# Flamingo-style decoder block: first three attentions with fp32 scores in row groups, a ones column in V, and DMA layout of later queries and keys

## The reference

```python
x = x + tanh(g_xattn[i]) * xattn_i(layernorm(x), ctx)   # i = 0..3
x = x + tanh(g_ffn[i])   * ffn_i(layernorm(x))
```

```python
q = heads((x @ Wq.T + bq) * 8**-0.5)      # attention 0 scales the scores, which is the same
k, v = heads(ctx @ Wk.T + bk), heads(ctx @ Wv.T + bv)
scores = q @ k.T + bias_i                 # 256 x 256 for each head and batch
scores = where(mask, scores, -inf)        # 0: an integer mask per query; 1, 2: key padding
out = (softmax(scores) @ v).merge_heads() @ Wo.T + bo
```

## Time and profile before

| | us |
|---|---|
| median of 3 runs | 860.76 (860.72 to 862.41) |
| profiled execution, its own time | 862.37 |
| its span | 860.4 |
| PE busy | 702.3 (82%) |
| DVE busy | 573.1 (67%) |
| ACT busy | 488.9 (57%) |
| POOL busy | 166.6 (19%) |
| DMA moved | 32.26 MB |

### The profile page before, as it was taken

One profiled execution on the slowest core, in us unless ns is written; L12 is line 12 of the kernel. 1 busy time (PEld: TensorE's weight loads), 2 busy tenths in 40 slices (PEclk: granted clock), 3 DMA queues, 4 the chain that ended last, 5 costly groups with the idle time before them and its releaser, 6 DMA issues. The chain is left out here.

```text
span 860.4 us, 14382 instructions
## 1 busy us (share of the span) xinstructions
PE 702.3 (82%) x4728; PEld 396.0 (46%) x4728; DVE 573.1 (67%) x1765; ACT 488.9 (57%) x1323; POOL 166.6 (19%) x135
## 2 busy tenths in 40 slices
PE   4589994559997878999744899949999999869978
PEld 2266663336665323333222667635336666644322
DVE  3699995869996358667865999855316666436553
ACT  2288881259883568598812988812666556413201
POOL 8622000420000045536655000020000000000000
PEclk8689997769999768998885999979999999969999
DMA  8895004060000000000009200000000000000000
GB/s 310 169 319 177 2 7 69 23 126 2 2 2 2 0 1 0 1 0 1 1 0 180 41 2 2 2 26 0 1 0 1 1 2 2 1 1 1 0 1 24
DMA packets 22056, 32.26 MB, mean 38 GB/s; under 512 B 1760, under 2 KB 15712, under 8 KB 21216
## 3 DMA queue, kind: packets, MB, share of 16 engines
q1 hardware_dynamic: 21984, 31.36, 14.4%
HBM read 21.39 MB, written 9.96 MB: 36 GB/s over the span
## 5 line engine op out<-in xcount | busy, mean ns | idle before, releaser
L816 ACT ACTIVATE RING<-RING,NMX 128x256 f32<-128x256 f32 x384 | 190.7, 500 | 56.2 <-DVE NMX L1637 55.8
L1637 DVE CUSTOM_DVE_ANT_0 RING<-bank,ADJM 128x256 f32<-128x256 f32 x384 | 143.4, 413 | 23.5 <-DMA scratch<-RING 22.5
L1158 PE MATMUL bank<-W,RING 128*128 128x128 f32 x768 | 120.5, 282 | 15.6 <-ACT RING L828 13.9
L541 POOL TENSOR_TENSOR small<-small 128x8 f32<-128x8 f32 (+2 forms) x13 | 17.7, 1365 | 463.1 <-DVE small L1528 463.1
L1158 PEld LDWEIGHTS bank<-W,RING 128*128 128x128 f32 x768 | 91.7, 145 | 27.9 <-ACT RING L816 23.2
L1138 PE MATMUL bank<-ARENA 128*128 128x256 bf16 x384 | 77.8, 290 | 30.7 <-DMA ARENA<-scratch 25.7
L1649 DVE COPY RING<-bank 128x512 f32<-128x512 f32 x144 | 98.6, 686 | 1.2 <-PE bank L1158 0.8
L816 ACT ACTIVATION_READ_ACCUMULATOR RING<-RING,NMX 128x1 f32 x384 | 72.8, 190 | 0.0
L997 PE MATMUL bank<-XT,W 128*128 128x512 f32 (+2 forms) x118 | 62.2, 668 | 6.6 <-ACT XT L712 5.3
L728 ACT ACTIVATE RING<-bank,NMX 128x512 f32<-128x512 f32 x64 | 43.4, 683 | 41.8 <-PE bank L1062 21.2
L1280 PE MATMUL bank<-ARENA,W 64*128 64x512 f32 x180 | 62.3, 710 | 3.6 <-DVE ARENA L1830 2.3
(11 more groups left out here) (253 smaller groups left out, 1307.3 us busy)
## 6 DMA issues: line engine op xcount, KB each, us to landing
scratch<-ARENA SPq DMA_DIRECT2D x18, 256.0 KB, 3.2
ARENA<-scratch SPq DMA_DIRECT2D x6, 768.0 KB, 10.6
W<-in_weights SPq DMA_DIRECT2D x1, 2564.0 KB, 21.2
scratch<-RING SPq DMA_DIRECT2D x36, 64.0 KB, 3.0
ARENA<-scratch SPq DMA_DIRECT2D x12, 192.0 KB, 3.8
scratch<-RING SPq DMA_DIRECT2D x18, 128.0 KB, 2.9
ARENA<-scratch SPq DMA_DIRECT2D x6, 384.0 KB, 6.6
W<-in_weights SPq DMA_DIRECT2D x2, 1024.0 KB, 13.7
```

Source lines behind the costliest of these rows:

```text
L816: nc.scalar.activation(P_OF(n)[:, q * S:(q + 1) * S], S_OF(n)[:, q, :], ACT.Exp, bias=NMX[:, 2 * t + q:2 * t + q + 1], scale=-1.0, accum_o ...
L1158: mm = nc.tensor.transpose(bk[:, o:o + P], P_OF(n)[:, i:i + P], ident)
L1637: nc.vector.tensor_tensor_reduce(out=S_OF(n)[:, q, :], in0=SBANK(n)[:, q * S:(q + 1) * S], in1=ADJM[:, b, q, :], scale=-1.0, scalar=BIG, o ...
```

## The change

- The bf16 parts, the DRAM scratch and all clearing of `QS` and `KS` go. Queries and keys stay fp32 in `QT` and `KT`: a head's 8 features lie in partitions 32j to 32j+7 of group g. The scores of a group for 128 queries are four fp32 products with 8 rows each, at rows 0, 32, 64 and 96, into banks 0 to 3. All four banks are used for one such step and again for the next. A unit `n` is now a pair of heads for 128 queries, so the count of units, of maxima and of exponentials stays.
- The queries and keys of the first 256 tokens (for keys, of attention 0 only) are produced in that layout by PE itself (`heads`, four column groups), with the biases spread by 16 small products (`biases`). Those of the later tokens are plain products into `QC` and `KC`, laid out by DMA within SBUF, 16 transfers of 8 rows (`scatter`). Their products are issued inside the loop at t = 1; V of attentions 0 and 2 at t = 3; the bias row of attention 0 at t = 5.
- V gets a column of ones for each head, so the product with V gives the row sums too. The sums in ACT's exponential go, as do L1654 and L1190. In their place: a copy of the 128 x 256 product by DVE, two transposes, a reciprocal straight from PSUM and a small product on DVE for each group; for each batch two transposes back, a copy by ACT, and one product (and bias row) for each 128 tokens with Wo gathered by 16 DMAs (`compact`).
- The copies of transposed probabilities alternate between DVE and ACT. The products with V are spread, one half of the keys at every other t.
- DVE makes only batch 0 of attention 0's masks ahead of the loop, and the others at t = 6 of the loop (`other_masks`), after a wait for the other masks, the padding and the bias matrices of attentions 1 and 2. Some of POOL's mask work for attentions 1 and 2 moves ahead of their layernorms.
- Keys of attentions 1 and 2, V and the bias row of 1, and the bias row of 2, are made during feed-forward part 0.

```diff
-LAG, PV_T, OTR_T, SEL_T, OUT_T = 3, 8, 9, 13, 27
-PT_SLOTS = 7
+LAG, PV_T, OTR_T, ONE_T, BACK_T, OUT_T, END_T = 3, 7, 9, 11, 25, 29, 14
...
-        QS = ARENA[:, 0:8192].bitcast(BF16).rearrange("p (h t) -> p h t", h=H16)
-        KS = ARENA[:, 8192:12288].bitcast(BF16).rearrange("p (j t) -> p j t", j=H16 // 2)
+        QT = ARENA[:, 0:4096].rearrange("p (g t) -> p g t", g=4)
+        KT = ARENA[:, 4096:8192].rearrange("p (g t) -> p g t", g=4)
+        PT = ARENA[:, 8192:12288].rearrange("p (s j k q) -> p s j k q", s=2, j=4, k=2)
...
-        def SBANK(n):
-            return bank[(0, 1, 7)[n % 3]]
-
         def TBANK(n):
-            return bank[(2, 3, 5)[n % 3]]
+            return bank[4 + n % 2]
...
+            def compact(a):
+
+                at = COL[f"wo{a}"][0]
+                for g in range(NG):
+                    for j in range(HG):
+                        sp.dma_start(WOC[a][PAD * g + DH * j:PAD * g + DH * (j + 1), :],
+                                     w_in[PAD * j:PAD * j + DH, at + g * P:at + (g + 1) * P]).then_inc(s_wo[a], 16)
+
+            def scatter(dst, src, t0, done):
+
+                for g in range(NG):
+                    for j in range(HG):
+                        r = PAD * g + DH * j
+                        sp.dma_start(dst[PAD * j:PAD * j + DH, g, t0:TOK], src[r:r + DH, t0:TOK]).then_inc(done[g], 16)
+
+            compact(0)
+            sp.wait_ge(s_he, NG + 2)
+            scatter(KT, KC[0], S, s_ks)
+            sp.wait_ge(s_ea, QC_AT[0])
+            scatter(QT, QC, S, [s_qs] * NG)
...
+            sp.dma_start(ADJ[:, 1:3, :, :], adj_in[:, 1:3, :, :]).then_inc(s_ldm2, 16)
...
+            sp.wait_ge(s_adjm, B * TPB)
+            compact(1)
+            sp.wait_ge(s_he, NG + 4)
+            scatter(KT, KC[1], 0, s_ks)
+            compact(2)
+            sp.wait_ge(s_ea, QC_AT[1])
+            scatter(QT, QC, S, [s_qs] * NG)
...
+            def clear_values():
+
+                nc.gpsimd.memset(ARENA[:, 14336:14336 + NT * VW], 1.0).then_inc(s_zero, 1)
+
             pool.wait_ge(s_set, 1)
             roots()
+            clear_values()
             pool.wait_ge(s_set, 2)
-            masks(0)
-            for a in (1, 2):
-                for step in range(4):
-                    key_parts(a, step)
+            masks(0, 1, B)
...
-                            nc.scalar.activation(P_OF(n)[:, q * S:(q + 1) * S], S_OF(n)[:, q, :], ACT.Exp,
-                                                 bias=NMX[:, 2 * t + q:2 * t + q + 1], scale=-1.0,
-                                                 accum_out=SUMS[:, 2 * t + q:2 * t + q + 1]
+                            nc.scalar.activation(P_OF(n)[:, i * S:(i + 1) * S], S_OF(n)[:, i, :], ACT.Exp,
+                                                 bias=NMX[:, 2 * t + i:2 * t + i + 1], scale=-1.0
...
+            def heads(out, name, g, rhs):
+
+                for j in range(HG):
+                    f = DH * (HG * g + j)
+                    mm = nc.tensor.matmul(out[PAD * j:PAD * j + PAD, :], w(name, f, f + PAD), rhs, start=True,
+                                          stop=True)
+                return mm
...
+                    if t < UNITS and t % 2 == 0:
+                        m = t // 2
+                        b, g, q = m // 8, m // 2 % 4, m % 2
+                        if q == 0 and b == 0:
+
+                            pe.wait_ge(s_qd if g % 2 else s_qa, 2 * a + g // 2 + 1)
+                            if a > 0:
+                                pe.wait_ge(s_ks[g], 16 * HG * (a + 1))
+                        if m == 8:
+                            pe.wait_ge(s_qs, 16 * H16 * (a + 1))
+                            if a == 0:
+                                for k in range(NG):
+                                    pe.wait_ge(s_ks[k], 16 * HG)
+                        scores.fill(pe, [(s_max, 2 * base + 4 * m + 4)])
+                        for j in range(HG):
+
+                            r = slice(PAD * j, PAD * j + DH)
+                            mm = nc.tensor.matmul(bank[j][:, 0:S], QT[r, g, b * S + q * P:b * S + (q + 1) * P],
+                                                  KT[r, g, b * S:(b + 1) * S], start=True, stop=True)
+                            if j % 2 == 1:
+                                mm.then_inc(s_s, 1)
+                    if t == 1:
+                        later_queries(a)
+                    if a != 1 and t == 3:
+                        values(a, ra, s_fa)
+                    if a == 0 and t == 5:
+                        out_row(0, ra, s_fa)
...
+                        for j in range(HG):
+
+                            f = PITCH * (HG * g + j)
+                            mm = nc.tensor.matmul(bank[6][PAD * j:PAD * j + PAD, 0:S], V[:, 2 * b + part, f:f + PAD],
+                                                  PT[:, GG % 2, j, part, :], start=(part == 0), stop=(part == 1))
...
+                    if t >= ONE_T and (t - ONE_T) % 4 == 0 and (t - ONE_T) // 4 < UNITS // 4:
+
+                        G = (t - ONE_T) // 4
+                        GG, b = base // 4 + G, B * a + G // 4
+                        pe.wait_ge(s_otr, GG + 1)
+                        pe.wait_ge(s_on, GG)
+                        if G % 4 == 0:
+                            pe.wait_ge(s_otn, b)
+                        if G % 4 == 1:
+                            pe.wait_ge(s_res, TPB * b)
+                        for q in range(TPB):
+                            mm = nc.tensor.transpose(bank[7][:, q * P:(q + 1) * P],
+                                                     OTR[:, GG % 2, q * P:(q + 1) * P], ident)
+                        mm.then_inc(s_one, 1)
+                    if t >= BACK_T and (t - BACK_T) % 16 == 0:
+
+                        b = (t - BACK_T) // 16
+                        i = B * a + b
+                        pe.wait_ge(s_on, 4 * i + 4)
+                        for q in range(TPB):
+                            mm = nc.tensor.transpose(bank[7][:, q * P:(q + 1) * P], ON[:, i % 2, q, :], ident)
+                        mm.then_inc(s_back2, 1)
...
+                            nc.tensor.matmul(o, OTN2[:, i % 2, q * P:(q + 1) * P], WOC[a], start=True, stop=False)
+                            mm = nc.tensor.matmul(o, ones_row, BOR[a], start=False, stop=True)
...
+            def other_masks():
+
+                dve.wait_ge(s_ldm2, 48)
+                mask_terms(1, B)
...
+                        if a == 0 and t == 6:
+                            other_masks()
...
+                        src = bank[7][:, 0:S].rearrange("p (q j r) -> p q j r", q=2, j=HG)
+                        link(nc.vector.reciprocal(RS, src[:, :, :, DH:PITCH]))
+                        nc.vector.tensor_tensor(
+                            ON[:, i % 2, :, PAD * g:PAD * g + PAD].rearrange("p q (j d) -> p q j d", j=HG),
+                            src[:, :, :, 0:DH], RS.to_broadcast([P, TPB, HG, DH]), ALU.mult).then_inc(s_on, 1)
...
```

More of the change, by code:

```diff
@@ L473, in write @@
-            def write(side, parts, slots, cut, ready, n_ready, written):
-                rows = scratch[side].rearrange("(h i d) t -> i h d t", h=H16, i=6)
-                for part in range(3):
-                    sp.wait_ge(ready, n_ready + part + 1)
-                    for i in slots[part]:
-                        sp.dma_start(rows[i][:, :, cut], parts[:, part, cut]).then_inc(written, 16)
-            def read(side, dst, cut, written, n_written, done):
-                sp.wait_ge(written, n_written)
-                rows = scratch[side].rearrange("(j e r) t -> e r j t", e=2, r=6 * DH)
-                for e in range(2):
-                    sp.dma_start(dst(e)[:, :, cut], rows[e][:, :, cut]).then_inc(done, 16)
@@ L545, in roots, with masks @@
                 root(TPB, NT)
-            def masks(a):
+            def masks(a, b0, b1):
                 if a > 0:
                     pool.wait_ge(s_max, 2 * UNITS * a)
-                for b in range(B):
+                for b in range(b0, b1):
                     for q in range(TPB):
@@ L609, in _ @@
             nc.gpsimd.partition_all_reduce(AMAXR, AMAX, P, bass.bass_isa.ReduceOp.max).then_inc(s_amr, 1)
+            pool.wait_ge(s_ldm2, 48)
+            masks(1, 0, 2)
             roots()
-            masks(1)
+            masks(1, 2, B)
             root()
@@ L693, in _ @@
             pool.wait_ge(s_int, 2 * NC)
-            clear_queries()
-            clear_rest()
+            clear_values()
             roots()
-            masks(2)
+            masks(2, 2, B)
             root()
@@ L829, in attention @@
[L829 to L837 removed]
+                        if GG >= 2:
+                            act.wait_ge(s_pv, GG - 1)
@@ L1013, in turn, with biases, first_keys, keys @@
                     n_xn[0] += 1
-            def keys(a):
-                for c in range(NC):
-                    product(rk, [(w(f"wk{a}"), CT[:, half(c)])], s_fk)
+            def biases():
+                at = COL["cols"][0] + CI["bk0"][0]
```

(31 more changed lines are left out.)

498 lines of the change are left out of this document (214 added, 284 removed).

## The result

The changed kernel takes 961.48 us (median of four executions, 949.41 to 988.53) against 860.86 beside it. That is 1.107 times the time before, with a 95% interval of 1.101 to 1.113. The forecast was 808 (786 to 838). The executions of the changed kernel differ far more among themselves than those of before, and their time goes with the granted clock (0.839 at 949.41 us, 0.784 at 988.53, and 0.774 in one more of 992.27). The profile shown is of the one of 988.53 us, with a span of 986.7.

What follows compares the result with a forecast made beforehand. DVE was taken to bound the attention loops, before and after. Savings of 13.1, 17.0 and 23.4 us in attentions 0, 1 and 2, less 1 in the feed-forward part, made -52.5 us: median 808 us, range 786 to 838.

Steps and rivals of the forecast that it cites:

- The first maxima at 24, about 160 and about 425 us: Sign of being right: when the loops of attentions 0, 1 and 2 take their first maximum.
- stop at t = 6: Attention 0's loop: DVE waits 9 us for the bias matrices, queued behind scatters, before making the other masks.
- rival 4: Loops: DMA layout late, every loop stops at m = 8, 5 us each; 823 us, chance 0.05.
- the 7.6 to 9.5 given: Ahead of each loop: us from first normalised tile to first maximum, 7.6 at the high clock, otherwise taken as 9.5.
- DVE bounds the loop of the kernel before: Attention loops before the change: DVE has about 21 us of work in a batch of 22.19 us.
- rival 2: Score products: row groups run one after another, 3.9 us a pair; 941 us, slower than before; chance 0.04.
- the step on ACT: Loop: ACT loses 32 accumulator reads a batch (190 ns each) and gains four copies; no gain of its own.
- 2.47 to 2.55 of my sum: Loop, us per pair of units: PE's work at 2.47 against DVE's at 2.55.
- PE's sum of 2.47 us a pair: Loop, PE: scores 0.68, transposes 0.86, V product 0.68, other transposes and output product 0.25.
- DVE as the bound at 20.4 a batch: Loop: DVE's work 19.7 us plus 0.7 waiting for the output product, saving 1.8 us a batch.
- rival 5: Score products: row groups overlap only in part, scores 0.87 us, PE bounds at 21.3 a batch; 819 us, chance 0.07.
- Rival 1: Loop: the single set of score banks makes PE and DVE take turns, 22 to 22.6 us a batch; 831, chance 0.24.

Runs made afterwards that it cites:

- e10: e6 with the V products and everything after them two steps of t later: 818.18 us, 0.948 times before.
- e1: The changed kernel with 32 rows instead of 8 in each score product, the added query rows zero, waits left alone: 892.68 us, 1.036 times before.
- e5: The changed kernel with 32-row score products and ACT's copy of transposed probabilities put ahead of the exponentials: 837.07 us, 0.972 times before.
- e6: e5 with the bias matrices of attentions 1 and 2 transferred early, ahead of the 32 issues: 828.49 us, 0.962 times before.
- e7: e5 with the V products and everything after them one step of t later: 896.11 us, 1.041 times before.
- e11: The changed kernel with 16 rows in each score product, 8 of them zero, as in e1: 919.02 us, 1.063 times before.
- e3: The changed kernel, still 8 rows, with ACT's copy of transposed probabilities put ahead of the exponentials: 842.53 us, 0.979 times before.
- e2: The kernel before with 8 rows instead of 128 in its bf16 score products, so scores differ: 901.58 us against 861.6 beside it.

## Why the prediction was wrong

*Right: what is outside the loops.* The first maxima at 24, about 160 and about 425 us were forecast with fast loops. The changed kernel has 21.0, and in e10, where the loops are fast, they are at 21.7, 155.9 and 425.4; e10 has no stop at t = 6, but its loops are a little longer than forecast. The DMA layout was never late (rival 4). From the tile at 221.71 to the maximum at 229.08 it is 7.4 us, a little under the 7.6 to 9.5 given. That DVE bounds the loop of the kernel before is not tested: no run takes work off DVE there. The row groups run side by side (rival 2): eight records in 0.71 us, where one after another they would take 1.9. (That 1.9 is from 3.75/4 = 0.94 for a record of 512 columns, which counts in the end of the last; the four start 0.85 apart, which gives 1.7.)

*Wrong, the step on ACT: "it was not the bound and gets further from it. No gain of its own."* It is busy less, and it still sets the pace, because of what stands in front of what in its queue. The change gave ACT every other copy of transposed probabilities, and I counted these as work. I did not follow the one instruction to who waits for it: the V product on PE, one unit later. In the new order the copy stands behind the exponentials of a pair whose scores have only just been made. Scores, maxima, exponentials, copy and V product are thus one chain each second pair: 4.08 us against the 2.47 to 2.55 of my sum. From e1 to e5 it is 55.6 us, at or near the full clock in both.

*Wrong, the clock, which was never a step.* Every duration of the loop's sum was read at 1.00, and I took it as given that a loop with PE nearly full keeps it. With 8 rows it did not: from the changed kernel to e1 it is 60.0 us. The miss of 145 us is thus 60.0 of clock, 55.6 of chain and 29 of sizes (below). In the other order the shares differ: with the copy first, the clock comes back too, and 110.2 of the 115.7 us between the changed kernel and e5 are gone. The chain is thus the main cause and the clock what makes it twice as dear; what in the chain lets the clock fall is not shown.

*Mis-sized: PE's sum of 2.47 us a pair, and DVE as the bound at 20.4 a batch.* e5, with neither trouble, is at 837, 29 us above the forecast, and 12 batches of 22.8 - 20.4 = 2.4 make 28.8. In its profile the three loops are 29.7 us above the forecast's 252.5 and all the rest is 4 us below the forecast, so that the match is partly luck. Of the 2.4, 1.3 are the wait of 0.25 us that is left in each second pair and what hangs on it, which e10 takes away (22.8 to 21.5; from e6 to e10 the loops lose 16 us, of which 10.3 are left in the time, since other stretches got longer). The other 1.1 are PE's: its sum of 2.47 made 19.8 a batch, safely under DVE's 20.4, and it is 21.5. I had 0.68 + 0.86 + 0.68 = 2.22 for a pair without the transposes of a group, and it takes 2.41; eight times 0.19 is 1.5 of the 1.7 missing. The timeline of e10 has 0.16 of the 0.19 at the transposes, eight in 1.02 us (97.10 to 98.12) where two times 0.43 was read; the V product with the next scores behind it takes 0.74 (95.72 to 96.46) and the scores 0.64, where both had 0.68. The size is that of rival 5, which had 2.41 with the same two terms beside 0.87 for the scores, 21.3 us a batch and 819. The starts of single records in the trace of e10 bear it out in part: the second four score records start 0.32 us after the first four, where the V product's, in column groups, start 0.24 after. The row groups overlap a little less, which would be worth 0.16 a pair, but how much of the miss is this and how much the changes of shape, of which there are three in such a pair, the records don't part.

The Trainium skill (TensorE: Matmul & The Clock Gate, Measured speedup vs the span model) has 3.07 times for four row groups of 32 rows and 512 columns. An estimate from it, 1.9/3.07 + 0.25 = 0.87 for the scores, gives 2.41 us for this pair, and the trace agrees with the sum (94.05 to 96.46 in e10), though not with the term, since from the scores to the transposes it has 0.64.

*The rivals.* Rival 1 (the single set of banks) does not bound the changed kernel: its score products wait 2.5 us for DVE in all. Its mechanism is real, and e7 shows its price once DVE has other work between the maxima: 59 us (837.07 to 896.11). None of the five named the reason that came. The one that I named on the slow side, the serial row groups, was excluded by a row, and I put no other in its place; a chance of 0.95 for faster rested on that.

## What to carry to other kernels

For each instruction that a change hands to another engine, write down who waits for it and what it stands behind there, even if that engine has time to spare; put a copy whose input is long ready ahead of work whose input has only just been started. Where two units share one step, delay a stage by a whole step, or its work falls between the parts of the other. And read the granted clock of a loop beside its busy share before durations of it are carried over to products of another shape.

## What the runs showed of the chip that I had not expected

- The granted clock didn't follow PE's busy share. With the same instructions in the same order it was 1.00 with PE busy 15.72 of 20 us at 32 rows in the score products (e1), 0.59 with 18.06 at 16 rows (e11) and 0.50 with 18.95 at 8 rows, each from 80 to 100 us. Part of the higher shares is the low clock itself, at which a record takes longer: from 310 to 330 us, at 0.97, the changed kernel has 15.71 too, and then falls back to 0.5. At 8 rows without the waits it was 1.00 with 18.80 (e3). In e1 the queries are zero in the added rows.
- The changed kernel is at both levels in the same loop code, 0.50 in one stretch and 0.97 in another, and its executions spread by over 4% where those of before beside e1, and those of e1, spread by under 0.4%. What moves it from one to the other these runs don't show.
- Two changes of the product's shape cost about 0.25 us a unit in e2 as well, where the scores are bf16 and nothing else in the unit changed.
